# Layer 0 of a two-layer GNN kernel: TensorE's order of products, and the sums of four blocks in single rounds

## The chip, the cores and the metric

The kernel runs on one core of a Trainium2 chip. The metric is the device time of one execution in microseconds (us). Engines: TensorE (PE; its weight loads are PEld), VectorE (DVE), ScalarE (ACT), GpSimd (POOL), and SyncE (SP), which only issues transfers.

## The reference

Two message-passing layers, each on a layer norm with a rectifier, with a residual. Sizes: 6250 nodes, 206250 edges, 64 features. The changed code computes the first layer:

```python
e = jnp.concatenate([x[row], x[col]], axis=-1)                  # 206250 x 128
g1 = _lrelu(jnp.einsum('ef,hgf->heg', e, gate_w1))              # 4 heads x 64
alpha = _lrelu(jnp.einsum('heg,hog->heo', g1, gate_w2))         # 4 heads x 1
a = w_edge * jnp.exp(alpha)
inv = 1.0 / segment_sum(a, row) + 1e-16
m1 = _lrelu(jnp.einsum('ef,hgf->heg', e, msg_w1))               # 4 heads x 128
beta = _lrelu(jnp.einsum('heg,hog->heo', m1, msg_w2))           # 4 heads x 64
out_h = segment_sum(a * inv[row] * beta, row)
return jnp.mean(out_h, axis=0)
```

## The kernel before, in words

A first stage sorts the edges by source and makes tables of node rows. Then layer 0 runs over `NB` = 404 blocks of 512 edges (`B`; `T` = 4 tiles of 128), layer 1 over the same number, and there is a short end. A flag (`fit`) chooses between two ways of each layer at run time; the profile shows the way with windows, whose functions end in `_windows`. Four blocks are a quad (`NQ` = 101): the edges of one block have their sources in 32 neighbouring nodes (`WIN0`), so the four blocks of a quad fill the 4 x 32 rows of one bank (`ps_sum`).

There is no planner: each engine has its own written order of work, and semaphores tie them. `fours` runs a body for blocks 0 to 3, then a hardware loop with four blocks a turn, then the last four. A block b goes like this:

- SP (`load0_windows`) loads the rows of the near ends' window and the block's indices (`dst_rows_sb`), two blocks ahead, after the first products of block b - 2; POOL gathers the far ends (`ends`) three blocks ahead, once the weights of four blocks before have been spread.
- PE transposes the far ends (`turn_far`, L1557), ACT copies them out twice (`copy_ends`, L859, L860), DVE makes the near ends' selection matrix (`match_near`, L1147).
- The first products: the hidden layer has `NK` = 6 chunks of 128 rows, two for the gates (0, 1) and four for the messages (2 to 5). A chunk is two fp32r matmuls into one of three banks (`first_product_windows`, L1568, L1569). ACT scales it by 0.2 (`scale_chunk`, L813) and DVE takes the maximum (`rectify_chunk_windows`, L1158) into `hidden[k]`. The product of chunk k waits until chunk k - 3 has been rectified.
- Gates: `gate_product` (L1602), `copy_gates` (L877), `turn_gates` (two transposes, L1611), `scale_alpha` (L882), the maximum `alpha` (DVE L1216), `exp_alpha` (L888), `spread_weights` (L1171).
- Messages, in two pairs of heads a = 0, 1: `pair_product` (L1620, bank `ps_beta[a]`) from two hidden chunks, `scale_pair` (L865), `rectify_pair` (L1163), back to edges by `turn_pair` (four transposes, L1628, into the same bank), `weigh_pair` (L1179).
- Sums: `match_src` (L1189) makes the selection by source; after the last block of a quad, `sum_quad` (L1639) does 4 rounds of 4 products, `copy_quad` (L872) copies the bank, and POOL adds it to the table in DRAM in four accumulating transfers (`add_rows`, L665), each of which waits until the one before has landed.

PE's order in block b (b' is the next block): chunks 2, 3; far ends of b'; pair 1 of b - 1 turned; chunk 4; gate product; pair product 0; chunk 5; chunk 0 of b'; gates turned; pair 0 turned; chunk 1 of b'; pair product 1; and, in the first block of a quad, `sum_quad` of the quad before.

A pair product waits for its hidden chunks and until the pair's bank has been weighed for the block before. A wait blocks all that stands behind it on the engine:

```python
pe.wait_ge(hidden_ready, NK * b + 2 * a + 4)
wait(pe, terms_ready, 2 * (b - 1) + a + 1)
```

## Time and profile before

| what | value |
|---|---|
| median of 3 runs | 6657.94 us (6652.79 to 6658.46) |
| the profiled execution, its own time | 6656.1 us |
| its span | 6654.2 us |
| PE / PEld busy | 4382.8 (66%) / 2598.3 (39%) |
| DVE busy | 4799.1 (72%) |
| ACT busy | 2634.2 (40%) |
| POOL busy | 3779.0 (57%) |

The span runs from the first to the last instruction. Layer 0's loop takes from about 670 to 4210 us; the stage of sorting is before it, layer 1 behind. Busy times hold the drain of each matmul, so the shares are averages over stages, and rows of the timeline are needed to see what waits. In a timeline, a row's second number is how long the instruction or group of instructions took, from its start to its end; the next may start before that, as engines are pipelined.

### The profile page before, as it was taken

The page shows a single profiled execution, that of the slowest core. Times are in us where ns is not written, and L with a number is a line of the kernel's source. Part 1 is how long each engine was busy: PE and PEld are TensorE (multiplying, and loading weights), DVE is VectorE, ACT ScalarE, POOL GpSimd, SP SyncE. Part 2 cuts the span into 40 slices and gives each one's busy share as a digit, 9 for nine tenths or more (in the row PEclk, how much of TensorE's full clock was granted, in tenths as well). Part 3 has the DMA queues.
Part 4 walks back from the last instruction along what each step waited for, and adds up shares of the span by engine and source line. Part 5 has one row for each costly group of instructions (what it writes and reads, how often), then busy time and mean ns, then how long its engine had stood idle before and what let it go on. Part 6 is the DMA issues. An engine that isn't in the chain of part 4 may idle for free.

```text
span 6654.2 us, 117791 instructions
## 1 busy us (share of the span) xinstructions
PE 4382.8 (66%) x24069; PEld 2598.3 (39%) x24069; DVE 4799.1 (72%) x10127; ACT 2634.2 (40%) x6054; POOL 3779.0 (57%) x3799
## 2 busy tenths in 40 slices
PE   3611999999999999999999999233333333333334
PEld 1211444444444444444444444133333333333333
DVE  6986788888888888888888888755555555555554
ACT  1200666666666666666666666200000000000000
POOL 0100555555555555555555555177777777777774
PEclk9955999999999999999999999655555555555555
DMA  8301333333333333333333333222222222222222
GB/s 237 152 0 33 73 72 72 72 72 72 72 72 72 72 72 72 72 72 72 71 71 72 72 71 72 70 51 50 51 50 51 51 50 51 50 51 51 50 51 59
DMA packets 485530, 452.11 MB, mean 68 GB/s; under 512 B 281672, under 2 KB 372041, under 8 KB 483593
## 3 DMA queue, kind: packets, MB, share of 16 engines
q0 software_dynamic: 137360, 180.87, 16.9%
q1 hardware_dynamic: 321118, 246.02, 13.3%
q10 hardware_dynamic: 27008, 24.74, 1.5%
q8 instruction: 14, 0.23, 0.0%
q14 instruction: 30, 0.25, 0.0%
HBM read 363.66 MB, written 87.55 MB: 68 GB/s over the span
## 4 chain that ended last, share of the span: by engine, by line
PE 27%; DVE 26%; issue 20%; POOL 19%; DMA 3%; ACT 3%; POOLq 1%; DVEq 1%; SPq 0%; ACTq 0%
POOL ends L749 11%; POOL work L749 8%; PE ps_beta L1620 6%; DVE work L1158 6%; PE ps_beta L1628 5%; PE ps_hidden L1568 5%; DVE work L1287 5%; PE ps_hidden L1569 4%; DVE beta L1163 4%; DVE ends_hot L1147 3%; PE ps_sum L1639 3%; DVE terms L1179 2%; ACT scaled L813 2%; DVE parts L1179 2%; PE ps_T L1557 1%
## 5 line engine op out<-in xcount | busy, mean ns | idle before, releaser
L1767 PE MATMUL ps_beta<-work,equal 128*128 128x128 f32 x3232 | 834.1, 440 | 1548.5 <-DVE work L1492 1548.5
L652 POOL DMA_INDIRECT ends<-split_table,src_sb x808 | 775.7, 960 | 1456.0 <-issue 1429.7
L1767 PEld LDWEIGHTS ps_beta<-work,equal 128*128 128x128 f32 x3232 | 719.4, 328 | 1663.4 <-issue 1523.3
L1158 DVE TENSOR_TENSOR work<-work,ps_hidden 128x512 f32<-128x512 f32 x1616 | 1099.7, 680 | 256.6 <-ACT work L813 256.0
L1568 PE MATMUL ps_hidden<-ends_parts,w_high 128*128 128x512 f32 x2424 | 1109.4, 458 | 1.2 <-ACT ends_hot L860 1.2
L813 ACT ACTIVATE work<-ps_hidden 128x512 f32<-128x512 f32 x1616 | 965.0, 597 | 325.1 <-DVE work L1158 316.0
L652 POOL DMA_INDIRECT ends<-split_table,gather_sb x808 | 805.5, 997 | 502.4 <-issue 374.6
L749 POOL DMA_INDIRECT work<-src_table,src_sb x808 | 814.8, 1008 | 336.6 <-issue 239.2
L749 POOL DMA_INDIRECT ends<-src_table,gather_sb x808 | 863.5, 1069 | 245.6 <-issue 245.3
L1620 PE MATMUL ps_beta<-work,msg_w_sb 128*64 128x512 f32 x3232 | 871.6, 617 | 192.8 <-DVE work L1158 192.8
L1569 PE MATMUL ps_hidden<-ends_hot,window 128*128 128x512 f32 x2424 | 958.9, 396 | 0.0
L992 ACT ACTIVATE gates<-dots 128x8 f32<-128x8 f32 x404 | 84.2, 209 | 2113.9 <-DVE dots L1473 2113.9
L1568 PEld LDWEIGHTS ps_hidden<-ends_parts,w_high 128*128 128x128 f32 x2424 | 456.2, 188 | 653.7 <-issue 452.6
L865 ACT ACTIVATE beta_scaled<-ps_beta 128x512 f32<-128x512 f32 x808 | 483.7, 599 | 551.3 <-PE ps_beta L1620 549.6
L1158 DVE TENSOR_TENSOR work<-scaled,ps_hidden 128x512 f32<-128x512 f32 x808 | 554.1, 686 | 186.3 <-ACT scaled L813 186.3
L1163 DVE TENSOR_TENSOR beta<-beta_scaled,ps_beta 128x512 f32<-128x512 f32 x808 | 554.4, 686 | 116.1 <-ACT beta_scaled L865 116.1
L813 ACT ACTIVATE scaled<-ps_hidden 128x512 f32<-128x512 f32 x808 | 484.3, 599 | 223.0 <-PE ps_hidden L1569 195.4
L1628 PE MATMUL ps_beta<-ident,beta 128*128 128x128 f32 x3232 | 524.6, 285 | 55.3 <-DVE beta L1163 31.4
L1486 DVE TENSOR_TENSOR work<-ends,gates 128x256 f32<-128x256 f32 x202 | 88.7, 439 | 589.4 <-DMA ends<-src_table,gather_sb 589.4
L1569 PEld LDWEIGHTS ps_hidden<-ends_hot,window 128*128 128x128 f32 x2424 | 460.2, 190 | 36.6
L1628 PEld LDWEIGHTS ps_beta<-ident,beta 128*128 128x128 f32 x3232 | 343.2, 140 | 190.1 <-DVE beta L1163 171.2
L665 POOL DMA_DIRECT2D sums<-key_rows x404 | 382.1, 946 | 42.6 <-ACT key_rows L872 22.4
(156 smaller groups left out, 6189.6 us busy)
## 6 DMA issues: line engine op xcount, KB each, us to landing
window<-window_table SPq DMA_DIRECT2D x808, 96.2 KB
dst_rows_sb<-by_src SPq DMA_DIRECT2D x404, 128.0 KB
window_table<-parts SPq DMA_DIRECT2D x50, 770.0 KB, 3.3
ends<-in_edge_attr SPq DMA_DIRECT2D x202, 128.0 KB
key_rows<-in_edge_attr SPq DMA_DIRECT2D x202, 128.0 KB
sums<-key_rows POOLq DMA_DIRECT2D x404, 32.6 KB
sums<-parts ACTq DMA_DIRECT2D x10, 1305.0 KB, 14.9
ends<-split_table,src_sb POOLq DMA_INDIRECT x808
```

The costliest lines, as they stand in the source:

```text
L652: pool.indirect_dma_start(out=ends[m][:, t, :], out_offset=None, in_=split_table, in_offset=bass.IndirectOffsetOnAxis(ap=src_windows[m][:, ...
L665: pool.dma_start(sums0[0][bass.ds(first, WIN0), :], quad_sum[m * WIN0:(m + 1) * WIN0, :], accum_op=ALU.add).then_inc(quad_added, 16)
L749: pool.indirect_dma_start(out=ends1_windows[m][:, t, :], out_offset=None, in_=src_table, in_offset=bass.IndirectOffsetOnAxis(ap=src_window ...
L813: nc.scalar.activation(scaled[k % NL][:, :], ps_hidden[k % NL][:, :], ACT.Copy, scale=SLOPE).then_inc(scaled_ready, 1)
L865: nc.scalar.activation(beta_scaled[:, a * B:(a + 1) * B], ps_beta[a][:, :], ACT.Copy, scale=SLOPE).then_inc(beta_scaled_ready, 1)
L1158: nc.vector.tensor_tensor(hidden[k][:, :], scaled[k % NL][:, :], ps_hidden[k % NL][:, :], ALU.max).then_inc(hidden_ready, 1)
L1163: nc.vector.tensor_tensor(beta_T[a], beta_scaled[:, a * B:(a + 1) * B], ps_beta[a][:, :], ALU.max).then_inc(beta_ready, 1)
L1568: nc.tensor.matmul(o, w1_high[:, k * P:(k + 1) * P], ends_parts[j][:, :], start=True, stop=False)
L1569: nc.tensor.matmul(o, window[j][:, k * P:(k + 1) * P], ends_hot[j][:, :], start=False, stop=True).then_inc(hidden_done, 1)
L1620: last = nc.tensor.matmul(ps_beta[a][i * D:(i + 1) * D, :], msg_w2_sb[:, 2 * a + i, :], hidden[2 + 2 * a + i][:, :], start=True, stop=True)
L1628: last = nc.tensor.transpose(ps_beta[a][:, t * P:(t + 1) * P], beta_T[a][:, t * P:(t + 1) * P], ident[:, :])
L1767: last = nc.tensor.matmul(ps_beta[0][0:WIN, 0:W1], hot[m % 2][:, t, :].bitcast(F32), terms1_windows[m][:, t, :], start=(m == 0 and t == 0) ...
```

## The change

All of it is in the way with windows of layer 0.

1. PE's order: the first products run as 2, 3, 4 and 5, 0, 1. Pair 0 is turned back in the next block, like pair 1. The pair products stand last.
2. `sum_quad` becomes `sum_round`: one of the four rounds in each block of the next quad, between the pair products.
3. For that, the terms and the selections of a quad have second buffers (`terms_quads`, `hot_quads`, in memory that is free then); PE and DVE run `quads`, a loop with eight blocks a turn, and the sums are copied and added a quad later (`fours_late`).
4. ACT and DVE follow the new order.

```diff
+        def quads(eng, body):
+            for quad in range(3):
+                for m in range(4):
+                    body(4 * quad + m, quad, m, quad % 2)
+            with eng.Fori(1, (NQ - 3) // 2) as i:
+                for odd in (1, 0):
+                    for m in range(4):
+                        body(8 * i + 8 - 4 * odd + m, 2 * i + 2 - odd, m, odd)
+            for quad in range(NQ - 2, NQ):
+                for m in range(4):
+                    body(4 * quad + m, quad, m, quad % 2)
...
 POOL, edges0_windows (fours_late; add_rows of quads NQ - 2 and NQ - 1 after the loop)
-                adds = m >= 2 and not first_four(b)
+                adds = m >= 2 and not first_two(quad)
-                    add_rows(quad - 1, 2 * m - 4)
+                    add_rows(quad - 2, 2 * m - 4)
...
 ACT, edges0_windows
-                if begun:
+                if not (isinstance(b, int) and b == 0):
+                    scale_alpha(b - 1)
                     scale_pair(b - 1, 1)
+                    exp_alpha(b - 1)
                 scale_chunk(b, 2)
-                if m == 1 and not first_four(b):
-                    copy_quad(quad - 1)
+                if m == 0 and not first_two(quad):
+                    copy_quad(quad - 2)
                 scale_chunk(b, 3)
+                scale_chunk(b, 4)
                 if not is_last(b):
                     copy_ends(b + 1, 1 - j)
-                scale_chunk(b, 4)
                 copy_gates(b)
-                scale_pair(b, 0)
                 scale_chunk(b, 5)
                 if not is_last(b):
                     scale_chunk(b + 1, 0)
-                scale_alpha(b)
+                scale_pair(b, 0)
                 if not is_last(b):
                     scale_chunk(b + 1, 1)
-                exp_alpha(b)
...
 DVE, edges0_windows (in the buffers' first user of a quad: wait(dve, summed, quad - 1) for quad)
                     rectify_pair(b - 1, 1)
                 rectify_chunk_windows(b, 2)
-                if begun:
-                    spread_weights(b - 1, before_quad, before_m)
-                    match_src(b - 1, before_quad, before_m)
-                    weigh_pair(b - 1, 0, before_m)
-                rectify_chunk_windows(b, 3)
                 if not is_last(b):
                     match_near(b + 1, half + j, 1 - j)
+                rectify_chunk_windows(b, 3)
                 if begun:
-                    weigh_pair(b - 1, 1, before_m)
+                    spread_weights(b - 1, before_quad, before_m, before_odd)
                 rectify_chunk_windows(b, 4)
-                rectify_pair(b, 0)
+                if begun:
+                    weigh_pair(b - 1, 0, before_m, before_odd)
+                    match_src(b - 1, before_quad, before_m, before_odd)
+                    weigh_pair(b - 1, 1, before_m, before_odd)
                 rectify_chunk_windows(b, 5)
                 if not is_last(b):
                     rectify_chunk_windows(b + 1, 0)
+                rectify_pair(b, 0)
...
 PE
-            def sum_quad(b, quad):
+            def sum_round(b, quad, t, odd):
+                if t == 0:
+                    pe.wait_ge(terms_ready, 2 * b + 2)
+                    pe.wait_ge(src_hot_ready, b + 1)
+                    wait(pe, quad_copied, quad)
+                for m in range(4):
+                    last = nc.tensor.matmul(ps_sum[m * WIN0:(m + 1) * WIN0, 0:W0], hot_quads[odd][m][:, t, :].bitcast(F32),
+                                            terms_quads[odd][m][:, t, :], start=(t == 0), stop=(t == T - 1))
+                if t == T - 1:
+                    last.then_inc(summed, 1)
...
                 first_product_windows(b, 2, half, j)
                 first_product_windows(b, 3, half, j)
+                first_product_windows(b, 4, half, j)
                 if not is_last(b):
                     turn_far(b + 1, quad + (m + 1) // 4, (m + 1) % 4)
                 if begun:
+                    turn_pair(b - 1, 0)
+                gate_product(b)
+                if begun:
                     turn_pair(b - 1, 1)
-                first_product_windows(b, 4, half, j)
-                gate_product(b)
-                pair_product(b, 0)
                 first_product_windows(b, 5, half, j)
                 if not is_last(b):
                     first_product_windows(b + 1, 0, half + j, 1 - j)
+                    first_product_windows(b + 1, 1, half + j, 1 - j)
                 turn_gates(b)
-                turn_pair(b, 0)
-                if not is_last(b):
-                    first_product_windows(b + 1, 1, half + j, 1 - j)
+                pair_product(b, 0)
+                if not first_four(b):
+                    sum_round(b - 1 - m, quad - 1, m, 1 - odd)
                 pair_product(b, 1)
-                if m == 0 and begun:
-                    sum_quad(b - 1, quad - 1)
```

## Rows read from the trace of the kernel before

**Rows 1.** One quad in a view of windows: span, then PE, PEld, DVE, ACT, POOL busy, PE clock, DMA share, GB/s.

```profile
3010.09:3045.14 35.05, 32.60 (x203) 17.17 (x201) 29.33 (x57) 24.15 (x53) 19.39 (x21) 1.00 0.34 70
```

**Rows 2.** What uses the banks `ps_hidden`: durations min/median/max in ns, first and last start.

```profile
L1568 PE MATMUL ps_hidden<-ends_parts,w_high x2424: 388/479/792, 669.9 to 4206.2; 128*128 128x512 f32 x187
```

**Rows 3.** TensorE's timeline, one block: start us, duration us, engine, line, operation.

```profile
3036.95 0.50 PE L1568 MATMUL ps_hidden<-ends_parts,w_high 128*128 128x512 f32 x1
...
3037.98 0.60 PE L1557 MATMUL ps_T<-ident,ends 128*128 128x128 f32 x4
3038.43 0.66 PE L1628 MATMUL ps_beta<-ident,beta 128*128 128x128 f32 x4
3038.84 0.47 PE L1568 MATMUL ps_hidden<-ends_parts,w_high 128*128 128x512 f32 x1
...
3039.49 0.64 PE L1602 MATMUL ps_alpha<-work,gate_w_sb 128*32 128x256 f32 x8
3040.57 1.08 PE L1620 MATMUL ps_beta<-work,msg_w_sb 128*64 128x512 f32 x4 [0.45 <-DVE work L1158]
3041.59 0.50 PE L1568 MATMUL ps_hidden<-ends_parts,w_high 128*128 128x512 f32 x1
...
3042.62 0.38 PE L1611 MATMUL ps_alpha<-ident,parts 128*128 128x128 f32 x2
3043.08 0.66 PE L1628 MATMUL ps_beta<-ident,beta 128*128 128x128 f32 x4
...
3044.13 1.08 PE L1620 MATMUL ps_beta<-work,msg_w_sb 128*64 128x512 f32 x4
```

**Rows 4.** TensorE's timeline around one quad's sums.

```profile
3025.84 1.08 PE L1620 MATMUL ps_beta<-work,msg_w_sb 128*64 128x512 f32 x4
3026.85 0.41 PE L1639 MATMUL ps_sum<-terms,equal 128*32 128x261 f32 x2
...
3028.75 0.50 PE L1568 MATMUL ps_hidden<-ends_parts,w_high 128*128 128x512 f32 x1
```

**Rows 5.** Waits, 2000 to 4000 us: total us, times, longest us.

```profile
DVE work L1158 <- ACT scaled L813: 106.1, 57, 1.9
```

**Rows 6.** VectorE's timeline, the same block.

```profile
3038.35 0.69 DVE L1158 TENSOR_TENSOR work<-scaled,ps_hidden 128x512 f32<-128x512 f32 x1
...
3040.55 0.54 DVE L1147 TENSOR_SCALAR ends_hot<-dst_rows_sb,window 64x512 fp32r<-64x512 int32 x1
...
3044.19 0.16 DVE L1216 TENSOR_TENSOR alpha<-alpha_scaled,ps_alpha 128x16 f32<-128x16 f32 x1
```

**Rows 7.** ScalarE's timeline, after that block's pair product 1.

```profile
3045.26 0.60 ACT L865 ACTIVATE beta_scaled<-ps_beta 128x512 f32<-128x512 f32 x1 [0.24 <-PE ps_beta L1620]
```

**Rows 8.** The match of near ends, 2000 to 4000 us: durations min/median/max in ns.

```profile
L1147 DVE TENSOR_SCALAR ends_hot<-dst_rows_sb,window x228: 534/616/707, 2005.9 to 3994.9; 64x512 fp32r<-64x512 int32 x114
```

**Rows 9.** Timelines of the index rows' loads, steady and first, and what waited.

```profile
3036.10 0.49 SPq L470 DMA_DIRECT2D dst_rows_sb<-by_src  x1
...
661.55 0.49 SPq L470 DMA_DIRECT2D dst_rows_sb<-by_src  x1
...
665.04 0.49 DVE L1147 TENSOR_SCALAR ends_hot<-dst_rows_sb,window 64x512 fp32r<-64x512 int32 x1 [41.46 <-DMA dst_rows_sb<-by_src]
```

**Rows 10.** The page's queues of instructions: packets, MB, share of 16 engines.

```profile
q8 instruction: 14, 0.23, 0.0%
q14 instruction: 30, 0.25, 0.0%
```

**Rows 11.** Timeline of layer 0's end, all engines.

```profile
4214.37 0.39 ACT L872 ACTIVATE key_rows<-ps_sum 128x261 f32<-128x261 f32 x1 [4.31 <-PE ps_sum L1639]
4215.57 0.76 POOL L665 DMA_DIRECT2D sums<-key_rows  x1 [17.54 <-ACT key_rows L872]
4217.09 1.28 ACT L968 ACT_TABLE_LOAD   x1 [2.33 <-issue]
...
4228.54 0.85 SPq L516 DMA_DIRECT2D parts<-sums  x2
```

More of the change, by code:

```diff
@@ L70 @@
 assert P * RUN >= EP and RUN == 4 * B and NP <= 1 << FIELD
-assert COPIES == 2 and NT % CH == 0 and NB >= 12 and ROWS * W0 % (P * 5) == 0
+assert NQ % 2 == 1 and COPIES == 2 and NT % CH == 0 and NB >= 12 and ROWS * W0 % (P * 5) == 0
 def gnn(nc, x, src, dst, src_rows, dst_rows, dst_all, edge_attr, edge_weight, node_vec, node_vec1, node_vec1_n2,
@@ L348, in fours, with fours_late, first_two @@
                 body(NB - 4 + m, NB // 4 - 1, m)
+        def quads(eng, body):
[9 more added lines that the diff above has]
+                    body(4 * quad + m, quad, m, quad % 2)
+        def fours_late(eng, body):
+            for b in range(8):
+                body(b, b // 4, b % 4)
+            with eng.Fori(2, NQ - 1) as i:
+                for m in range(4):
+                    body(4 * i + m, i, m)
+            for m in range(4):
+                body(NB - 4 + m, NQ - 1, m)
         def early(b):
             return isinstance(b, int) and b < 2
+        def first_two(quad):
+            return isinstance(quad, int) and quad < 2
         def first_four(b):
@@ L677, in edges0_windows @@
                 if adds:
-                    add_rows(quad - 1, 2 * m - 3)
+                    add_rows(quad - 2, 2 * m - 3)
             pool.wait_ge(tail_step, 2)
@@ L693, in _ @@
                 pool.wait_ge(zeroed, 16 * 5 * COPIES)
-                fours(pool, edges0_windows)
-                for m in range(4):
-                    add_rows(NQ - 1, m)
+                fours_late(pool, edges0_windows)
+                for quad in range(NQ - 2, NQ):
+                    for m in range(4):
+                        add_rows(quad, m)
                 pool.wait_ge(quad_added, 64 * NQ)
@@ L955, in _ @@
                 scale_chunk(0, 1)
-                fours(act, edges0_windows)
+                fours_late(act, edges0_windows)
+                scale_alpha(NB - 1)
                 scale_pair(NB - 1, 1)
+                exp_alpha(NB - 1)
+                copy_quad(NQ - 2)
                 copy_quad(NQ - 1)
@@ L1164, in rectify_pair, with spread_weights, weigh_pair @@
                                         ALU.max).then_inc(beta_ready, 1)
-            def spread_weights(b, quad, m):
+            def spread_weights(b, quad, m, odd):
                 dve.wait_ge(exp_ready, b + 1)
                 if m == 0:
-                    wait(dve, summed, quad)
-                nc.vector.tensor_tensor(terms_quad[m][:, :, H * D:H * D + H], alpha_exp[:, :, :],
+                    wait(dve, summed, quad - 1)
+                nc.vector.tensor_tensor(terms_quads[odd][m][:, :, H * D:H * D + H], alpha_exp[:, :, :],
                                         ends[m][:, :, 2 * D:2 * D + 1].broadcast_to([P, T, H]),
                                         ALU.mult).then_inc(weight_ready, 1)
-            def weigh_pair(b, a, m):
+            def weigh_pair(b, a, m, odd):
                 dve.wait_ge(beta_turned, 2 * b + a + 1)
@@ L1378, in _ @@
             with dve.If(fit):
+                dve.wait_ge(row_out[0], 16 * ((NT + 1) // 2))
+                dve.wait_ge(row_out[1], 16 * (NT // 2))
+                dve.wait_ge(tables_split, 32)
+                for m in range(4):
+                    nc.vector.memset(terms_quads[1][m][:, :, W0 - 1:W0], 1.0).then_inc(ones_set, 1)
                 match_near(0, 0, 0)
@@ L1381, in _ @@
                 rectify_chunk_windows(0, 1)
-                fours(dve, edges0_windows)
+                quads(dve, edges0_windows)
                 rectify_pair(NB - 1, 1)
-                spread_weights(NB - 1, NQ - 1, 3)
-                match_src(NB - 1, NQ - 1, 3)
-                weigh_pair(NB - 1, 0, 3)
-                weigh_pair(NB - 1, 1, 3)
+                spread_weights(NB - 1, NQ - 1, 3, 0)
+                match_src(NB - 1, NQ - 1, 3, 0)
+                weigh_pair(NB - 1, 0, 3, 0)
+                weigh_pair(NB - 1, 1, 3, 0)
             with dve.Else():
@@ L1630, in turn_pair, with edges0_windows @@
                 last.then_inc(beta_turned, 1)
-            def sum_quad(b, quad):
-                pe.wait_ge(terms_ready, 2 * b + 2)
-                pe.wait_ge(src_hot_ready, b + 1)
-                wait(pe, quad_copied, quad)
-                for t in range(T):
-                    for m in range(4):
-                        last = nc.tensor.matmul(ps_sum[m * WIN0:(m + 1) * WIN0, 0:W0], hot_quad[m][:, t, :].bitcast(F32),
-                                                terms_quad[m][:, t, :], start=(t == 0), stop=(t == T - 1))
-                last.then_inc(summed, 1)
-            def edges0_windows(b, quad, m):
+            def sum_round(b, quad, t, odd):
[3 more added lines that the diff above has]
+                    wait(pe, quad_copied, quad)
+                for m in range(4):
+                    last = nc.tensor.matmul(ps_sum[m * WIN0:(m + 1) * WIN0, 0:W0], hot_quads[odd][m][:, t, :].bitcast(F32),
+                                            terms_quads[odd][m][:, t, :], start=(t == 0), stop=(t == T - 1))
+                if t == T - 1:
+                    last.then_inc(summed, 1)
+            def edges0_windows(b, quad, m, odd):
                 half, j = 2 * quad + m // 2, m % 2
@@ L1735, in _ @@
                 first_product_windows(0, 1, 0, 0)
-                fours(pe, edges0_windows)
+                pe.wait_ge(ones_set, 4)
+                quads(pe, edges0_windows)
+                turn_pair(NB - 1, 0)
                 turn_pair(NB - 1, 1)
-                sum_quad(NB - 1, NQ - 1)
+                for t in range(T):
+                    sum_round(NB - 1, NQ - 1, t, 0)
             with pe.Else():
```

26 lines of the change are left out of this document (14 added, 12 removed).

## The prediction

> **What bounds the kernel now.** I read the page's slices first, then one window of four blocks, then the timelines of TensorE, VectorE and ScalarE over that window, last the waits and the end of layer 0. The changed code runs in layer 0 alone: its 2424 first products start between 669.9 and 4206.2 us, so a block of six takes (4206.2 − 669.9) / 2423 × 6 = 8.757 us over 404 blocks [rows 2]. One quad (four blocks) lasts 35.05 us; in it PE is busy 32.60 us, DVE 29.33, ACT 24.15, POOL 19.39, and the granted clock is 1.00, the upper level [rows 1]. No engine is full: PE looks it, but its busy time holds the drain of each matmul. So I count occupancy, from one start to the next.
>
> A block without the quad's sums takes about 8.2 us. TensorE in it: chunks 2 and 3 together 3036.95 to 3037.98, 1.03; transposing the far ends 0.45; transposing pair 1 0.41; chunk 4 alone 0.65; the gate product, 0.64 to its last end, I take 0.50 of occupancy; pair product 0 1.02; chunks 5 and 0 1.03; turning the gates 0.22 (half of four transposes at 0.45); transposing pair 0 0.41, then chunk 1 alone 0.64 (3043.08 to 3044.13 holds both, 1.05); pair product 1 1.02 [rows 3]. Sum 7.38. So it waits about 0.8: before pair product 0 (0.45 is shown, after the rectified chunk 3) and 0.24 before pair 0's transposes, whose rectification has only just ended. The block is a ring: pair product 1, ScalarE's scaling, VectorE's pair 1, chunk 2, spread, match, weigh and chunk 3, pair product 0, its scaling and rectification, its transposes, chunk 1, pair product 1.
>
> Once a quad the sums add 3026.85 to 3028.75, 1.90 us of TensorE in one piece [rows 4]. VectorE has nothing to eat then: in 2000 to 4000 us it waited 106.1 us in 57 times (once a quad) for the scaled chunk, up to 1.9 us each [rows 5]. The mean of (4 × 7.38 + 1.90) / 4 = 7.86 against 8.757 leaves 0.90 of waiting a block on TensorE.
>
> VectorE: from chunk 2 to the start of alpha, 3038.35 to 3044.19, eleven operations follow without a gap, 5.84; with alpha (0.10), chunk 1 and pair 1 (0.60 each) it needs 7.14 a block [rows 6].
>
> **The change, part by part.**
>
> First products in threes. Alone, a chunk costs 0.65; in a pair 1.03 / 2 = 0.52, so each of a pair is 0.47 and each run of fp32r matmuls between fp32 ones costs 0.1 on the way in, and as much on the way out to a gate or pair product [rows 3]. Runs go from four (2 3, 4, 5 0, 1) to two (2 3 4 and 5 0 1), each ending in transposes: 2 × (1.03 + 0.47) = 3.00 against 1.03 + 0.65 + 1.03 + 0.64 = 3.35. Removed: 0.35 a block.
>
> Single rounds. The 1.90 becomes 0.48 in every block, between the pair products. TensorE's total is unchanged; VectorE is never without a chunk for 1.9 us.
>
> TensorE's new ledger: 3.00 + 0.45 + 2 × 0.41 + 0.50 + 0.22 + 2 × 1.02 + 0.48 = 7.51. Three borders are in no row: transposes to gate, turned gates to pair product 0, sums to pair product 1. The nearest rows are the way out of a run, 0.1, and the way from a pair product into the sums, none (3025.84 to 3026.85 is 1.01, as before a first product) [rows 4]. So 0 to 0.3; a little gain is excluded, since nothing can take less than its columns. I take 0.15: 7.66.
>
> Transposes back in the next block. Pair 0's are queued after chunk 4 of the next block. Pair product 0 starts at about 5.2 of a block and ends at 6.2; its scaling (0.05 to begin, 0.60 long [rows 7]) and rectification (0.68) are over about 7.6, the transposes come at 7.66 + 1.95 = 9.6. Both waits of the old ring are gone, by 2 us. Pair 1: product over at 7.7, scaled at 8.4, rectified by 9.1, turned at 10.5.
>
> What is late next. I walk VectorE in the new order, with pair product 0's end as 0: pair 0 starts at 0.70 and occupies 0.60; alpha now needs ScalarE's scaled alpha, queued behind chunk 1 (0.05 + 0.49 + 0.49 + 0.18 = 1.21), so it starts at 1.3; chunk 1 to 2.0; pair 1 needs the scaling of pair product 1, which ends about 2.15, so 2.2 to 2.8; chunk 2 (0.1 of waiting for ScalarE, which has scaled alpha, pair 1 and the exponential first) to 3.5; the match of near ends, 0.68 with its borders, to 4.2; chunk 3 4.8; spread 4.9; chunk 4 5.5. Chunk 1 of the next block needs that chunk 4: 0.47 + 0.22 + up to 0.1 + 1.08 gives the next pair product 0's end at 7.4. That is this ring, under TensorE's 7.66 by 0.25. Weigh pair 0 (to 6.1) is before its pair product (6.3), weigh pair 1, match and chunk 5 (to 7.5) before pair product 1 (8.0). VectorE carries 7.14 and three forced waits, about 0.4: 7.54. ScalarE has its 24.15 us a quad [rows 1], 6.04 a block, room in 7.66, and the same operations. The three are close; each upset of one is paid. The match lasts 534 to 707 ns, median 616 [rows 8], longer beside POOL's gathers, and POOL's share rises from 19.39 / 35.05 = 55% to 63%: 0.02 a block more, off TensorE's path while the 0.25 lasts. I add 0.04: 7.70 a block.
>
> Loads. SyncE's window loads follow chunk 5, the match of near ends now stands before chunk 3. Before: the index rows are issued at 3036.10, matched at 3040.55, 4.45 later [rows 6, 9]. Chunk 5 to the match shortens by some 0.8, so 3.6; the first such load took 661.55 to 665.04, 3.49 [rows 9]. It fits, by little; if not, 0.1 to 0.5 a block on VectorE. In the steady part DMA is busy 0.34 [rows 1], and I take 0. POOL's gathers start on the weights' spread, one chunk later than before, and are needed two blocks on: nothing. The four additions of a quad are spread over two blocks, as before.
>
> Ends. Four memsets more and a wait for tables written long before: under 1 us. At the end two quads are to be added instead of one. Before: the copy at 4214.37, the first addition at 4215.57, all landed before SyncE reads at 4228.54, 12.97 [rows 11]. Now quad 99's copy can start about 5 us earlier against the last product (it needs no final sums), and quad 100's copy waits for its four additions: one chain more of 13, less some 3: +10.
>
> Sum: 404 × (8.757 − 7.70) = 427, less 10: 417 us off this execution's 6656.1, 6239; its median of three runs is 1.8 higher, so 6240.
>
> **A rule on streamed code.** The loops of TensorE and VectorE grow from four blocks to eight. In this execution the instruction queues moved 14 and 30 packets in all [rows 10], over 99 turns of the loops of five engines: a turn fetches nothing. A TensorE body of four blocks has 203 matmuls and 201 weight loads [rows 1], the new one some 810 with its waits above that. The Trainium skill, "Runtime: NRT & Kernel Launch", section "Instruction fetch mechanics", says that a sequencer's store is a FIFO refilled in blocks of 256 instructions, 2048 of them for TensorE and 512 for the others, and that a taken branch to a target outside the window stalls. By it TensorE's body fits still, and VectorE's may straddle a block more than fits; what it would cost is rival B. A turn of before agrees with it (no fetch); no row shows an eight-block body.
>
> **Rivals.**
> A. VectorE keeps its waits. In before it waits 8.2 − 7.14 = 1.05 a block even without the sums; alpha behind chunk 1, pair 1 behind ScalarE, and a match that waits for its load could hold as much. For: three waits of 0.1 to 0.2 are forced in my walk already, and each upset runs through both engines. Against: none of them is longer than 0.2 there. Period 8.19: 404 × 0.567 − 10 = 219 off, 6437.
> B. One far jump a turn. Leaving layer 0's loop, ScalarE stands 2.33 us for nothing that the profile shows, ahead of its table load [rows 11]. 49 turns × 2.33 = 114: 6354. For: the body doubles. Against: no packet in any turn of before [rows 10].
> C. Slower than before. TensorE's eight-block body of over 810 instructions is streamed anew in each turn, and the engine stands at each piece instead of once. Place: the branch back, and each border of 256 instructions. It decides from 417 / 49 = 8.5 us a turn, 3.7 stops of 2.33. With five, 49 × 5 × 2.33 = 571: 6240 + 571 = 6811. Against: the same rows as for B, and a border crossed in order can be fetched ahead.
> D. TensorE's borders cost nothing and the rings slip under it: 7.51, or VectorE's 7.54: 404 × 0.16 = 65 better, 6175. It is the lower part of my own range.
> That the change does not do what it says (rounds or second buffers that still wait): the first round of a quad needs pair 1 of the block before weighed, at 6.9 in my walk, and starts after 7.4; its buffer is filled again a block after its last round. Weighing would have to slip by 0.5; this is part of A.
>
> **How the numbers follow.** Forecast with D, period 7.45 to 7.95: 0.65 (6140 to 6340). A and what lies between it and me: 0.19. B: 0.08. C: 0.05. No gain within 0.2% (about what a measurement of this kernel can tell from no change, 13 us): 0.02; faster than 6140: 0.01. The range to leave 2 in 10 out must reach over B and most of A, and below to a TensorE without borders and a little more: 6140 to 6430. Faster 0.92, same 0.02, slower 0.06 (C and the like of it).
>
> **What would show it.** A quad of 30.8 us; no 1.9 us wait of VectorE's once a quad; each run of three first products 1.5 us; no wait of TensorE's before pair product 0 and before either set of transposes; chunk 4's rectification over 0.1 to 0.3 before chunk 1's product starts; no instruction packets in the loop; two chains of additions at the end. Wrong if TensorE waits for chunk 1, 4 or 5's rectification by more than 0.3 a block, if VectorE waits on the index rows, or if something recurs every eight blocks.

## The result: slower, 6900 us where 6240 was forecast

The changed kernel takes 6900.49 us (6888.55 to 6903.65, 4 runs) against 6656.14 us (6652.79 to 6658.46, 4 runs) for the one before: ratio 1.0364, 95% interval 1.0346 to 1.0382. The forecast was 6240, in 6140 to 6430, with 0.06 on slower.

The line that uses the banks `ps_hidden` answers to [rows 2]; then layer 0 in a view of windows (its columns as in [rows 1]), and the page's granted clock and instruction queues, which answer to [rows 10]:

```profile
L1605 PE MATMUL ps_hidden<-ends_parts,w_high x2424: 388/397/796, 664.5 to 4435.7; 128*128 128x512 f32 x187
```

```profile
2000.00:2400.00 400.00, 361.34 (x2116) 195.60 (x2114) 306.23 (x593) 246.65 (x563) 204.06 (x211) 0.91 0.30 67
```

```profile
PEclk9955999999999999999999999855555555555555
...
q8 instruction: 22, 0.36, 0.0%
q14 instruction: 34, 0.28, 0.0%
```

(4435.7 − 664.5) / 2423 × 24 = 37.35 us a quad, where before had 35.03. The median matmul became shorter (397 ns against 479), and yet every engine is busy for less of its time than in [rows 1], and the granted clock is 0.91 instead of 1.00. Something stands still, for all engines at once. Three timelines show it: TensorE's from an undisturbed block into the stall, ScalarE's and POOL's over the stall.

```profile
3006.01 0.50 PE L1605 MATMUL ps_hidden<-ends_parts,w_high 128*128 128x512 f32 x1
...
3007.51 0.60 PE L1594 MATMUL ps_T<-ident,ends 128*128 128x128 f32 x4
3007.94 0.60 PE L1665 MATMUL ps_beta<-ident,beta 128*128 128x128 f32 x4
3008.47 0.64 PE L1639 MATMUL ps_alpha<-work,gate_w_sb 128*32 128x256 f32 x8
3009.04 0.66 PE L1665 MATMUL ps_beta<-ident,beta 128*128 128x128 f32 x4
3009.45 0.48 PE L1605 MATMUL ps_hidden<-ends_parts,w_high 128*128 128x512 f32 x1
...
3010.00 0.40 PE L1605 MATMUL ps_hidden<-ends_parts,w_high 128*128 128x512 f32 x1
...
3010.92 0.38 PE L1648 MATMUL ps_alpha<-ident,parts 128*128 128x128 f32 x2
3011.24 1.08 PE L1657 MATMUL ps_beta<-work,msg_w_sb 128*64 128x512 f32 x4
3012.24 0.65 PE L1676 MATMUL ps_sum<-parts,equal 128*32 128x261 f32 x8
3012.82 1.08 PE L1657 MATMUL ps_beta<-work,msg_w_sb 128*64 128x512 f32 x4
3013.83 0.50 PE L1605 MATMUL ps_hidden<-ends_parts,w_high 128*128 128x512 f32 x1
...
3017.59 0.40 PE L1606 MATMUL ps_hidden<-ends_hot,window 128*128 128x512 f32 x1
3021.50 0.79 PE L1605 MATMUL ps_hidden<-ends_parts,w_high 128*128 128x512 f32 x1 [3.50 <-ACT ends_hot L889]
...
3023.92 1.98 PE L1657 MATMUL ps_beta<-work,msg_w_sb 128*64 128x512 f32 x4
```

```profile
3014.64 0.59 ACT L842 ACTIVATE scaled<-ps_hidden 128x512 f32<-128x512 f32 x1
3018.93 0.39 ACT L901 ACTIVATE key_rows<-ps_sum 128x261 f32<-128x261 f32 x1 [3.69 <-DMA sums<-key_rows]
3019.22 1.08 ACT L842 ACTIVATE work<-ps_hidden 128x512 f32<-128x512 f32 x2
3020.17 0.62 ACT L888 ACTIVATE ends_parts<-ps_T 128x512 fp32r<-128x512 f32 x1
3020.65 0.59 ACT L889 ACTIVATE ends_hot<-ps_T 64x512 fp32r<-64x512 f32 x1
```

```profile
3004.57 0.94 POOL L693 DMA_DIRECT2D sums<-key_rows  x1
...
3008.11 0.95 POOL L693 DMA_DIRECT2D sums<-key_rows  x1
...
3012.55 0.95 POOL L693 DMA_DIRECT2D sums<-key_rows  x1
...
3016.57 0.90 POOL L693 DMA_DIRECT2D sums<-key_rows  x1 [0.43 <-issue]
```

From 3006.01 to 3013.83 a block takes 7.82 us, with no wait of TensorE's. Then ScalarE reaches the copy of a quad's sums (L901, `copy_quad`) at 3015.24 and stands until 3018.93. The copy writes the one buffer `quad_sum`, from which the four additions of the quad before are read, and `copy_quad` therefore waits for `quad_added` to reach 64 × quad. The last of them was issued at 3016.57; the chain of waits gives it 2.34 us:

```profile
3016.57 2.34 DMA sums<-key_rows
```

Behind the copy stand the scaling of chunks 3 and 4 and the copy of the far ends, which TensorE wants for chunk 0 of the next block: it idles 3.50 us to 3021.50. (A second matmul of a chunk is followed 0.23 later by the next; so the next was due at 3017.82 and comes 3.68 late.) After that idling it is granted less, as a view of windows shows (length, then PE, PEld, DVE, ACT and POOL busy, the granted clock, DMA share, GB/s):

```profile
3015.00:3018.00 3.00, 2.99 (x25) 1.84 (x23) 1.53 (x3) 0.24 (x1) 1.87 (x2) 1.00 0.20 44
3018.00:3021.00 3.00, 0.00 (x0) 0.00 (x0) 1.16 (x3) 2.07 (x5) 0.00 (x0) 0.84 0.36 77
3021.00:3024.00 3.00, 2.50 (x8) 1.69 (x10) 2.75 (x6) 1.59 (x4) 2.04 (x2) 0.50 0.24 66
3024.00:3027.00 3.00, 3.00 (x14) 0.57 (x16) 0.49 (x2) 0.98 (x3) 1.90 (x2) 0.52 0.21 47
3027.00:3030.00 3.00, 3.00 (x16) 1.88 (x15) 2.43 (x6) 2.20 (x7) 0.00 (x0) 1.00 0.09 19
```

A clock of 0.50 is the lower of the two levels, 1.2 GHz. From chunk 0 to the start of pair product 1 TensorE takes 5.36 us (3021.50 to 3026.86). In the block ahead the same operations take 2.82 (3010.00 to 3012.82), and 0.1 more where a run starts with them: 2.4 lost. Sum: 4 × 7.82 + 3.7 + 2.4 = 37.4, the measured quad. It is no accident of one quad: of the waits from 2000 to 4000 us (total, times, longest), two occur 54 times, once in each of the 2000 / 37.35 = 54 quads:

```profile
ACT key_rows L901 <- DMA sums<-key_rows: 201.4, 54, 4.2
...
PE ps_hidden L1605 <- ACT ends_hot L889: 190.7, 54, 4.0
```

### The profile page after: what moved, and what is told of

Its sections match the earlier page's. It is cut to its first block, busy times and chain, and to the rows that moved or that the text cites. A ratio compares the mean times of both kernels' runs of the same rounds, so it can differ in the third digit from the quotient of the medians.

```text
span 6898.2 us, 117345 instructions
## 1 busy us (share of the span) xinstructions
PE 4519.1 (66%) x24069; PEld 2719.8 (39%) x24069; DVE 4757.8 (69%) x10131; ACT 2542.7 (37%) x6054; POOL 3809.5 (55%) x3799
## 4 chain that ended last, share of the span: by engine, by line
PE 34%; POOL 23%; issue 19%; DVE 10%; DMA 7%; ACT 4%; POOLq 3%; ACTq 0%; DVEq 0%; SPq 0%
POOL ends L778 10%; PE ps_beta L1657 9%; POOL work L778 7%; PE ps_hidden L1605 6%; PE ps_hidden L1606 5%; DMA sums<-key_rows 4%; DVE work L1319 4%; POOL ends L680 4%; PE ps_beta L1665 3%; PE ps_sum L1676 2%; DVE work L1189 2%; PE ps_alpha L1639 2%; PE ps_T L1594 1%; POOLq L686 1%; PE ps_alpha L1648 1%
## 5 line engine op out<-in xcount | busy, mean ns | idle before, releaser
L1605 PE MATMUL ps_hidden<-ends_parts,w_high 128*128 128x512 f32 x2424 | 1094.9, 452 | 347.1 <-ACT ends_hot L889 346.2
L1606 PE MATMUL ps_hidden<-ends_hot,window 128*128 128x512 f32 x2424 | 1001.9, 413 | 0.0
L1657 PE MATMUL ps_beta<-work,msg_w_sb 128*64 128x512 f32 x3232 | 963.3, 677 | 0.2 <-DVE parts L1210 0.2
L842 ACT ACTIVATE work<-ps_hidden 128x512 f32<-128x512 f32 x1616 | 917.5, 596 | 82.6 <-PE ps_hidden L1606 82.4
L1605 PEld LDWEIGHTS ps_hidden<-ends_parts,w_high 128*128 128x128 f32 x2424 | 479.6, 198 | 793.9 <-DVE work L1189 387.1
L1606 PEld LDWEIGHTS ps_hidden<-ends_hot,window 128*128 128x128 f32 x2424 | 486.1, 201 | 71.0
L1665 PE MATMUL ps_beta<-ident,beta 128*128 128x128 f32 x3232 | 507.8, 280 | 0.8 <-DVE beta L1194 0.8
L1665 PEld LDWEIGHTS ps_beta<-ident,beta 128*128 128x128 f32 x3232 | 358.4, 141 | 168.0 <-issue 166.0
## 6 DMA issues: line engine op xcount, KB each, us to landing
sums<-key_rows POOLq DMA_DIRECT2D x404, 32.6 KB
```

What stands on the lines that cost most here:

```text
L842: nc.scalar.activation(scaled[k % NL][:, :], ps_hidden[k % NL][:, :], ACT.Copy, scale=SLOPE).then_inc(scaled_ready, 1)
L1605: nc.tensor.matmul(o, w1_high[:, k * P:(k + 1) * P], ends_parts[j][:, :], start=True, stop=False)
L1606: nc.tensor.matmul(o, window[j][:, k * P:(k + 1) * P], ends_hot[j][:, :], start=False, stop=True).then_inc(hidden_done, 1)
L1657: last = nc.tensor.matmul(ps_beta[a][i * D:(i + 1) * D, :], msg_w2_sb[:, 2 * a + i, :], hidden[2 + 2 * a + i][:, :], start=True, stop=True)
L1665: last = nc.tensor.transpose(ps_beta[a][:, t * P:(t + 1) * P], beta_T[a][:, t * P:(t + 1) * P], ident[:, :])
```

## The experiments

The theory (W): the wait of the copy for the additions costs 3.7 us a quad by itself and 2.4 by the clock; the rest of the change works. (C) in the expectations says that the serial additions bound the quad wherever they stand. The rivals: the new order or the rounds themselves are slower, or the longer loops are. Chips differ, so each ratio is against the kernel before on the same chip: 6660.18 us for the first four runs, 6839.87 for the next four, 6905.23 for the last four. The first of these is within 0.1% of the 6656.14 beside which the changed kernel took 6900.49; on the other two it is 2.7% and 3.7% slower. "A quad" is reckoned as above, from the first and the last start of the first products.

**1. Additions one block earlier.** `e1_adds_early`:

```
-                adds = m >= 2 and not first_two(quad)
+                adds = m in (1, 2) and not first_two(quad)
...
-                    add_rows(quad - 2, 2 * m - 4)
+                    add_rows(quad - 2, 2 * m - 2)
```

> GpSimd's four additions of a quad stand in its second and third block instead of its third and fourth; all else as in the changed kernel. Theory W (the copy of the sums, now in a quad's first block, waits on ScalarE until the last addition of the quad before has landed, 3.7 us, and TensorE then works at half clock for 5 us, 2.4 us more): in the changed kernel a quad is (4435.7 - 664.5) / 2423 x 24 = 37.35 us, its undisturbed blocks 7.82; without the wait 4 x 7.82 = 31.3, so 101 x 6.07 = 613 us less, 6287, granted clock 1.00 all through layer 0. Rival C (the four serial additions bound the quad wherever they stand, the wait only moves): above 6600. Rival P (the clock falls because of the fuller order of products, not because of the wait): some 3.7 us of the 6.07 come back, about 6525, and the clock stays near 0.91.

6292.16 us (6289.75 to 6297.28), ratio 0.9447 (0.9432 to 0.9463). A quad takes 31.31. Its windows and its line of first products:

```profile
2000.00:2400.00 400.00, 400.00 (x2553) 225.20 (x2552) 368.07 (x717) 295.92 (x677) 247.50 (x257) 1.00 0.36 80
```

```profile
L1605 PE MATMUL ps_hidden<-ends_parts,w_high 128*128 128x512 f32 x2424 | 1033.8, 427 | 2.0 <-ACT ends_hot L889 1.2 <-DVE work L1189 0.5
```

TensorE is busy all 400 us at full clock, and before its 2424 first products it idled 2.0 us in all (347.1 in the changed kernel). The loss is gone, as W expected (6287); C (above 6600) and the rival that blamed the clock on the new order (6525) are refuted. In one quad of its timelines the last addition is issued at 3013.48 and the copy starts at 3019.76, 6.3 later: with 2.34 for landing, 3.9 to spare.

**2. The same wait removed another way.** `e2_two_sums` leaves the additions late and gives the sums a second buffer, so that a copy waits for the additions of two quads before and for the first of the quad before, no longer for the last:

```
-                wait(act, quad_added, 64 * quad)
-                nc.scalar.activation(quad_sum[:, :], ps_sum[:, 0:W0], ACT.Copy).then_inc(quad_copied, 1)
+                wait(act, quad_added, 64 * (quad - 1) + 16)
+                nc.scalar.activation(quad_sums[odd][:, :], ps_sum[:, 0:W0], ACT.Copy).then_inc(quad_copied, 1)
```

> The additions stay where the changed kernel has them; instead the copied sums have a second buffer, so that a copy waits for the additions of two quads before. ScalarE and GpSimd run eight blocks a turn for that, as TensorE and VectorE do. W: the same as with early additions, 6287 within 15 us, since the additions have a whole quad to land. Rival C: above 6600. If loops of eight blocks on all engines cost something (a far jump once a turn, 49 turns x 2.33 us at most), it is up to 114 us slower than the kernel with early additions.

6289.42 us (6287.97 to 6293.65), ratio 0.9441 (0.9425 to 0.9456): the same as the first. Two edits that share nothing but the wait they take away give one time. That the wait costs the 610 us, its sequel included, is shown, and doubling ScalarE's and POOL's bodies to eight blocks cost nothing that the times show.

**3 and 4. Each half alone.** `e3_order_only` is the kernel before with the new orders of the four engines (products in threes, pair messages last, transposes a block later), sums still in one piece. `e4_rounds_only` has the rounds, the second buffers and early additions, in the old orders.

TensorE's part of the first (against the kernel before) and of the second (against the changed one); the other engines follow suit:

```
+                first_product_windows(b, 4, half, j)
...
-                    turn_pair(b - 1, 1)
-                first_product_windows(b, 4, half, j)
+                    turn_pair(b - 1, 0)
...
+                if begun:
+                    turn_pair(b - 1, 1)
```

```
-                first_product_windows(b, 4, half, j)
...
-                    turn_pair(b - 1, 0)
...
+                first_product_windows(b, 4, half, j)
+                gate_product(b)
+                pair_product(b, 0)
...
+                turn_pair(b, 0)
```

> The kernel before with the new order of products on TensorE, ScalarE and VectorE, but the quad's sums in one piece, single buffers and loops of four blocks, copy in the second block and additions as before. Ledger theory: a block without sums is 7.82 - 0.58 = 7.24 on TensorE, a quad 4 x 7.24 + 1.90 = 30.9 if VectorE's slack covers the piece, 32.4 if it is starved by 1.5 us: 6656 - 101 x (35.03 - 30.9 or 32.4) = 6239 to 6390. No wait for an addition, clock 1.00. Rival R (the single rounds are what makes the new order work; without them most of the gain goes): above 6450.

> The other half: second buffers, loops of eight blocks and single rounds (one behind each block's second pair product), with the early additions, but the orders of the kernel before on all engines. The ring of before, 8.19 a block, goes through TensorE's pair product 1 and not through the sums, so a round of 0.48 to 0.58 is partly beside it: 8.2 to 8.7 a block. 6656 - 101 x (35.03 - 32.8 to 34.8) + 13 for the second chain of additions at the end = 6444 to 6646; I expect 8.35, 6505. Rival (the order is what counts and the rounds give nothing): 6650 or more.

Order alone: 6322.32 us (6318.33 to 6330.46), ratio 0.9495 (0.9479 to 0.9511), a quad 31.71. Rounds alone: 6715.98 (6710.93 to 6724.0), ratio 1.0082 (1.0065 to 1.0099), a quad 35.50. The first lies in its range (6239 to 6390). The second is a miss: 6505 was expected, at most 6646, and its rival (the rounds give nothing without the order) came true. So the new order brings nearly all, and the rounds in the old order cost 56 us, where I had expected them to win 150. Their lines of waits say why, the first of e3 and the second of e4, both from 2000 to 4000 us:

```profile
DVE work L1160 <- ACT scaled L813: 84.4, 59, 1.6
```

```profile
PE ps_beta L1655 <- DVE work L1187: 121.0, 225, 0.7
```

With the new order the sums in one piece still hold VectorE up once a quad, as in [rows 5]. In the old one TensorE still waits before pair product 0 (121.0 / 225 = 0.54 each). My reading, which no further run tested: there the round of 0.58 lies on the ring that already bound the block, and is paid four times, where the piece of 1.9 was paid once. The gains do not add: −338 and +56 make −282, and together they give −368.

**5. Keep TensorE working through the wait.** `e5_filler` puts fifteen idle first products in front of chunk 5 in the block with the copy; they write a bank that is overwritten next.

```
+                if m == 0 and not first_two(quad):
+                    wait(pe, hidden_ready, NK * b + 3)
+                    for _ in range(15):
+                        nc.tensor.matmul(ps_hidden[2][:, :], w1_high[:, 0:P], ends_parts[j][:, :], start=True, stop=True)
```

> The changed kernel, its wait for the last addition untouched; in a quad's first block TensorE does 15 more fp32r products (128x128 on 128x512, 0.23 us each, 3.5 us) into the bank that chunk 5 is about to overwrite, so it works through the time in which it stood. Their results are used by nobody. Separates the 3.7 us of waiting from the 2.4 us of half clock after it. Theory W: the granted clock stays 1.00, the ScalarE wait stays, a quad is 31.3 + 3.7 = 35.0 instead of 37.35: 101 x 2.4 = 240 us less than the changed kernel, 6660, although TensorE does more. Rival (the clock falls for another reason, or the 15 products push the rest back by their own length): 6900 or more.

7129.67 us (7126.05 to 7141.73), ratio 1.0423 (1.0405 to 1.044), where the changed kernel had 1.0364 on another chip. The granted clock is 1.00 throughout, as expected, and yet the 240 us that were to come back are not in the ratio. Two lines of its waits, 2000 to 3600 us:

```profile
ACT beta_scaled L894 <- remote: 201.9, 82, 2.9
...
ACT key_rows L901 <- DMA sums<-key_rows: 147.5, 41, 4.6
```

The first is new: ScalarE stands twice a quad before a pair's scaling, for a releaser that the profile does not name. This run cannot be read without the changed kernel on the same chip, hence the repeats below.

**6. The late additions put into the kernel before.** `e6_before_late_adds`:

```
-                adds = m >= 2 and not first_four(b)
+                late = 1 if m == 3 else 2
+                adds = (m == 3 and not first_four(b)) or (m == 0 and not first_two(quad))
```

> The kernel before, only its additions moved one block later (the fourth block of a quad and the first of the next), so that the last of them stands one block before the copy, as in the changed kernel. Theory W: the same wait appears in an otherwise untouched kernel, 2 to 3.7 us a quad and as much as 2.4 us of half clock: 6656 + 101 x (2 to 6) = 6860 to 7260; I expect 6950. If the changed kernel's loss came from its order, its loops of eight blocks or its second buffers, this kernel stays at 6660 to 6675 (the last additions only).

6927.39 us (6917.9 to 6938.65), ratio 1.0129 (1.0111 to 1.0148), a quad 36.50. A miss in size and in mechanism: ratios of 1.03 to 1.09 were expected (6860 to 7260 with the kernel before at 6656), and from 2000 to 3600 us the copy waited in five quads only, 2.1 us in all. Here the last addition is issued 2.6 us before the copy (3018.94 and 3021.59 in one quad), just more than it needs to land, where in the changed kernel it is issued 1.3 us after ScalarE has reached the copy (3016.57 and 3015.24). So this run does not bear on W. The 87 us came through other waits between ScalarE, VectorE and TensorE, which I did not trace to one cause.

**7. Last addition one gather earlier.** `e7_half_wait`:

```
-                    gather0_tiles((m + 3) % 4, T // 2)
+                    gather0_tiles((m + 3) % 4, T // 2, 1 if split else 2)
...
+                if more and split:
+                    gather0_tiles((m + 3) % 4, T - 1, 1)
```

> The changed kernel with the last addition of a quad moved ahead by one gather (about 1.3 us earlier of the 3.7 us that ScalarE waits). Theory W: 101 x 1.3 = 130 us less for the wait alone, 6770; if the shorter stop also spares TensorE part or all of the half clock, up to 2.4 us more a quad, down to 6530. Rival C (additions bound the quad, their order does not matter): 6900.

7165.26 us (7152.41 to 7168.74), ratio 1.0478 (1.0461 to 1.0496). A miss: 130 us less than the changed kernel was expected. The wait stayed at 147.8 / 41 = 3.6 us, because the last addition was not issued earlier. It comes 8.7 us after the transposes of block 3's far ends, in the changed kernel on the same chip 8.8 (runs 11 and 9 below, means of 15 quads). It must wait until the one ahead has landed, and GpSimd now stood for that; the changed kernel has no such line (2000 to 3600 us):

```profile
POOL sums L693 <- DMA sums<-key_rows: 35.9, 25, 1.8
```

So within block 3 the chain of additions sets when the last one lands, and to move the last alone is not enough; the first experiment moves the whole chain.

**8. Rounds behind the gate product.** `e8_rounds_at_gates` is the first experiment with each round in the middle of the next block, where TensorE goes from the gates into transposes.

```
+                if m == 0:
+                    if not first_two(quad):
+                        sum_round(b - 5, quad - 2, 3, odd)
+                elif not first_four(b):
+                    sum_round(b - 1 - m, quad - 1, m - 1, 1 - odd)
```

> The kernel with early additions, and each round of sums moved from between the pair products to behind the gate product (both have 32 columns of weights), one block later, copy behind the gates' copy. TensorE is without any wait at 7.82 a block there, so every border saved counts: sums to pair product 1 (0.1) goes, 0.04 of the sums' own may: 7.70 a block, 6292 - 404 x 0.12 = 6244. VectorE's and ScalarE's ring was 7.54 a block in the kernel with the new order alone, so it is no bound yet. Rival (the border only moves to the way into the transposes of pair 1): 6290.

6585.42 us (6581.8 to 6590.79), ratio 0.963 (0.9614 to 0.9647), where 6244, or 0.938, was expected. It ran on a chip where the kernel before itself took 2.7% longer, and the first experiment did not run there, so this run does not tell what moving the rounds costs or gives. One wait in VectorE came up that the first experiment does not show (2000 to 3600 us):

```profile
DVE ends_hot L1178 <- DMA dst_rows_sb<-by_src: 23.5, 38, 1.1
```

This is the load that the prediction called short by little. It belongs to this kernel as much as to the chip: the filler, on the same chip, waited for it 3.4 us in all.

**9 to 12. The changed kernel, the filler, the half wait and the rounds at the gates, on one chip.**

> The changed kernel as it is, as the reference for the three kernels beside it: the runs of the filler, the moved addition and the moved rounds shared a chip on which the kernel before took 6840 us instead of 6657, and on which ScalarE showed a second wait (2.0 to 2.8 us, released by no engine of this core in the profile) after the wait for the additions. If that wait belongs to the chip, it is here too, in the changed kernel. Expected against the kernel before of the same chip: 1.036, as at first; 1.07 or more on the chip of the filler's runs.

> The kernel with 15 products in TensorE's gap, again, now with the changed kernel on the same chip. Theory W (2.4 of the 6.07 us of a quad are half clock): 101 x 2.4 = 240 us less than the changed kernel if the products fit the gap, and granted clock 1.00; each quad in which they don't fit costs the difference. Rival (the products push chunk 5 back and cost as much as the clock gives): the same as the changed kernel within 30 us.

> The last addition one gather earlier, again, with the changed kernel beside it: 130 us less than the changed kernel for 1.3 us of wait a quad, up to 370 less if the half clock goes too. Rival C (the additions bound the quad): the same as the changed kernel.

> Early additions, rounds behind the gate product, again: 0.963 of the kernel before on the first chip, where match of near ends waited for its index rows (38 times in 1600 us). If that wait is the chip's, on a chip where the kernel before takes 6657 the ratio is 0.938 (7.70 a block); if it is the kernel's, 0.963 there too.

The changed kernel 7208.8 (ratio 1.0437; 1.042 to 1.0455), filler 7179.42 (1.0396; 1.0378 to 1.0413), half wait 7195.99 (1.0418; 1.0401 to 1.0436), rounds at the gates 6639.23 (0.9611; 0.9595 to 0.9627). Against the changed kernel on this chip the filler wins 29 us, where W expected 240 and its rival at most 30, and the half wait 13, where 130 was expected. The rounds at the gates have the ratio that they had on the other slower chip, and wait for the index rows here too (19.1 us in 29 times), the changed kernel hardly (0.9 us in all); as the first experiment ran on neither chip, what they owe to the chip stays open. In windows of the changed kernel and then of the filler:

```profile
2400.00:2800.00 400.00, 354.12 (x2058) 186.06 (x2057) 296.97 (x577) 237.53 (x547) 198.83 (x205) 0.94 0.29 65
```

```profile
2400.00:2800.00 400.00, 376.91 (x2232) 208.92 (x2234) 298.67 (x582) 238.63 (x549) 204.51 (x211) 1.00 0.30 65
```

The clock did come back (0.94 to 1.00), and VectorE and ScalarE did hardly more in the same 400 us. Where the gain went shows when the quad is cut into its blocks, from one transposition of far ends to the next (means of the quads from 2000 to 3600 us):

| block | changed, first chip | changed, here | filler, here |
|---|---|---|---|
| with the copy | 14.07 | 13.31 | 11.52 |
| next | 7.83 | 7.83 | 9.31 |
| third | 7.82 | 9.73 | 10.01 |
| fourth | 7.82 | 7.86 | 7.86 |

In the block with the copy the filler wins 1.8 us, and what is left of the loss there, 11.52 − 7.83 = 3.7, is the wait alone (147.2 / 41 = 3.6). So the split of W holds where the copy stands: the wait costs its own length, and the clock 1.8 us here and 14.07 − 7.83 − 3.7 = 2.5 on the first chip, near the 2.4 of the single stall. The filler gives it back in the next two blocks, 1.5 and 0.3 us. There ScalarE stands for the unnamed releaser, in the changed kernel (first line) once a quad, with the filler (second line) twice (2000 to 3600 us):

```profile
ACT beta_scaled L894 <- remote: 109.9, 41, 2.9
```

```profile
ACT beta_scaled L894 <- remote: 209.8, 83, 2.9
```

The changed kernel has this wait on this chip and not on the first; it lies in the third block, which takes 9.73 us here and 7.82 there. What releases it is open, and so is whether the filler caused the second one.

## Why the prediction was wrong

**The step that failed** is a clause: "The four additions of a quad are spread over two blocks, as before." They are, in blocks 2 and 3 of a turn; but the diff moves `copy_quad` from block 1 to block 0. Against the additions it comes a block earlier, and a block itself became shorter. The wait on `quad_added` stands in the unchanged `copy_quad`, so no line of the diff shows it, and I priced the copy at nothing because its instruction is the same. The rows to price it with were there: an addition is issued behind two gathers each, in [rows 11] four additions have landed 12.97 us after the first is issued, some 3.2 each, and the last is the last thing that POOL issues in block 3. In the kernel before, the last addition and the copy that waits for it are 11.06 us apart:

```profile
3018.43 0.50 PE L1568 MATMUL ps_hidden<-ends_parts,w_high 128*128 128x512 f32 x1
```

```profile
3018.95 0.95 POOL L665 DMA_DIRECT2D sums<-key_rows  x1
```

```profile
3030.01 0.38 ACT L872 ACTIVATE key_rows<-ps_sum 128x261 f32<-128x261 f32 x1
```

Of this the block that the copy moved ahead, with the quad's sums in it, takes 10.3 (3018.43 to 3028.75 [rows 4]), which leaves 0.7 us for a landing of 2.3: a wait of 1.6. The other 2 us come from a second clause that priced something at nothing: "POOL's gathers start on the weights' spread, one chunk later than before, and are needed two blocks on: nothing." The additions stand behind those gathers. Before, the first gather of block 3 starts 3.00 us after the block's chunk 2 (3010.09 to 3013.09) and the last addition 0.5 us into the next block; in the changed kernel 4.24 (3006.01 to 3010.25) and 2.7 (3013.83 to 3016.57). That sharing out is reckoned from one quad of each trace; no run tested it by itself. None of the three signs that the prediction set for being wrong is the one that came, a wait of TensorE's for the copied far ends, once every four blocks.

Together the wait and its sequel cost (37.35 − 31.31) × 101 = 610 us, against the 608.7 by which the two spans (6898.2 and 6289.5) differ.

**What held**, read in the changed kernel's undisturbed blocks and in the first experiment:

TensorE's ledger. Runs of three take 1.50 and 1.47 (3006.01 to 3007.51, 3009.45 to 3010.92), forecast 1.5 each. The borders, put at 0 to 0.3 and taken as 0.15, measured 0.31: 7.82 against 7.51. Transposing pair 0 takes 0.53 where 0.41 stood, turning the gates 0.32 for 0.22, the sums 0.58 for 0.48. This mis-sized term is most of what the first experiment is above the forecast: (0.31 − 0.15 − 0.04 for the match) × 404 = 48 us of 6292 − 6240 = 52. Rival D, borders for nothing, is refuted by the same rows.

The waits. No wait before pair product 0 nor before either set of transposes. In the first experiment VectorE has no wait for a scaled chunk in 2000 to 3600 us; its short waits for a pair's scaling stay off the path (TensorE is busy 400.00 of 400). Rival A is refuted: a quad of 31.31 is not 4 × 8.19.

Loops of eight blocks. The instruction queues moved 22 and 34 packets, 8 and 4 more than in [rows 10], for 49 turns: nothing is fetched in a turn, and rivals B and C are refuted. C had the right sign, by luck, as its cause is not what slowed the kernel. The Trainium skill, "Runtime: NRT & Kernel Launch", section "Instruction fetch mechanics", has a taken branch to a target outside the window stall; this trace shows no such stall with TensorE's body of some 810 instructions and its waits, and none in the second experiment with ScalarE's and POOL's bodies doubled.

The index rows. VectorE did not wait for them in the changed kernel as first run or in the first experiment; a load issued at 3004.34 is matched at 3008.13, 3.8 us later for the forecast 3.6.

The tail. Two chains of additions, as forecast; the second copy waits for the first chain:

```profile
4440.15 0.38 ACT L901 ACTIVATE key_rows<-ps_sum 128x261 f32<-128x261 f32 x1
4452.81 0.39 ACT L901 ACTIVATE key_rows<-ps_sum 128x261 f32<-128x261 f32 x1 [12.27 <-DMA sums<-key_rows]
```

```profile
4465.04 0.85 SPq L544 DMA_DIRECT2D parts<-sums  x2
```

From the last first product to SyncE's read: 4465.0 − 4435.7 = 29.3, before 4228.5 − 4206.2 = 22.3: +7 for a forecast of +10. These rows also show the failed step in the open: the copy of a quad cannot start before the last addition of the one ahead has landed. I used that to price the tail and not the loop.

**The chances.** 0.06 for slower was too little for a change with five moved steps, since each move shifts waits whose text stays as it was. The mechanisms that I had put a price on held; a list of every wait on every moved instruction would have shown this one.

## What to carry to other kernels

When a diff moves an instruction, write down each semaphore that it waits on, and for each the block in which it is raised, before and after; the wait itself is not in the diff. A small copy in an in-order queue can stop every engine: here 0.39 us of ScalarE's work waited 3.7 us, and that with its sequel took 9% of the kernel's time (610 / 6898), and moving the additions by one block turned 3.6% slower into 5.5% faster. Read the tail of the trace, where dependences stand without overlap: what is serial there is serial in the loop too.

## What the runs showed of the hardware

An addition to `sums` in memory takes 2.34 us from its issue to the release of its waiter, and a chain in which each waits for the one ahead advances by 2.9 to 3.0 us (4447.69 to 4450.56 below, 2.87; 3.35 behind the first of a chain), for 32.6 KB each:

```profile
4447.69 0.76 POOL L693 DMA_DIRECT2D sums<-key_rows  x1 [2.23 <-DMA sums<-key_rows]
4450.56 0.76 POOL L693 DMA_DIRECT2D sums<-key_rows  x1 [2.11 <-DMA sums<-key_rows]
```

The Trainium skill, "DMA: Bandwidth & Descriptors", section "Anatomy of one DMA — SWDGE (gpsimd) path", gives each DMA that GpSimd issues a nearly constant cost of about 2 us, most of it the receipt of the write. The row of 2.34 agrees with the sum; no row here shows how it is made up.

TensorE stood still for 3.5 us and was then granted 0.50 and 0.52 of full speed from 3021 to 3027, and 1.00 after that. Three borders between kinds of matmul that before did not have (transposes to the gate product, turned gates to pair product 0, the sums to pair product 1) cost 0.31 us together, about 0.1 each. And one program took 6660, 6840 and 6905 us on three occasions, each on its chip within 0.3%: a per cent between kernels is to be had only on one chip. The ratio does not cure it, as the same pair of kernels gave 1.0364 on one chip and 1.0437 on another, whose changed kernel has a wait that the first does not show.
